# Graph layer and mixture of experts on one core: the results of the late tiles are scattered by node and choice and loaded with plain DMAs, and the first flush moves ahead by two slots

## The reference, cut to what matters

```python
def _L0_gnn_ref(h, edge_index, W, b):
    msg_sum = segment_sum(h[src], dst, num_segments=n)      # n = 6250 nodes, 100000 edges, rows of 256
    deg = segment_sum(ones, dst, num_segments=n)
    agg = msg_sum / maximum(deg, 1.0)[:, None]
    return concatenate([h, agg], axis=1) @ W.T + b

def _L0_ffn_ref(x, gamma, beta, Wr, br, W1, b1, W2, b2):
    xn = layernorm(x) * gamma + beta
    top_vals, top_idx = top_k(xn @ Wr + br, 2)              # 8 experts, each node goes to 2
    w = softmax(top_vals)
    for e in range(E):
        y_e = gelu(xn @ W1[e] + b1[e]) @ W2[e] + b2[e]      # 256 -> 512 -> 256
        y = y + y_e * w_full[..., e, None]
    return y

x = x + _L0_gnn_ref(_layernorm(x), edge_index, W, b)
x = x + _L0_ffn_ref(_layernorm(x), ...)
```

## Time and profile before

| | us |
|---|---|
| runs: median of 3 | 1417.49 (1415.44 to 1422.76) |
| profiled execution | 1415.15 |
| its span, first to last instruction | 1413.9 |
| busy: PE / DVE / ACT / POOL | 1139.6 / 809.4 / 462.6 / 950.6 |

### The profile page before, as it was taken

How to read it: one execution, slowest core, us unless ns; L and a number is a source line. 1 busy time by engine, 2 the same in 40 slices (tenths; PEclk the granted TensorE clock), 3 DMA queues, 4 the chain that set the end, 5 groups by cost and what they waited for, 6 DMA issues and landing times.

```text
span 1413.9 us, 23187 instructions
## 1 busy us (share of the span) xinstructions
PE 1139.6 (81%) x5743; PEld 878.7 (62%) x5743; DVE 809.4 (57%) x2583; ACT 462.6 (33%) x1017; POOL 950.6 (67%) x995
## 2 busy tenths in 40 slices
PE   3478798679768889888889988898898787899990
PEld 2234545457436767677767866776676566689980
DVE  8766645645644465555456546555776765652443
ACT  6200004113202433432252342343324333366650
POOL 3577777777777777777767776767675574205776
PEclk9999998889978999999999999999999988999995
DMA  8734655344334544444444543544444343235775
GB/s 269 231 107 135 215 182 167 118 131 136 117 119 128 153 131 146 144 136 140 141 128 127 151 139 121 152 123 132 153 139 117 111 136 98 78 110 156 227 222 150
DMA packets 125797, 205.43 MB, mean 145 GB/s; under 512 B 24491, under 2 KB 91844, under 8 KB 125540
## 3 DMA queue, kind: packets, MB, share of 16 engines
q0 software_dynamic: 48352, 129.18, 31.4%
q1 hardware_dynamic: 77188, 74.77, 16.2%
q10 hardware_dynamic: 128, 0.00, 0.0%
HBM read 160.19 MB, written 43.65 MB: 144 GB/s over the span
## 4 chain that ended last, share of the span: by engine, by line
PE 56%; DVE 14%; issue 10%; POOL 9%; ACT 7%; DMA 3%; DVEq 2%; ACTq 0%; POOLq 0%
PE psum L716 16%; PE psum L813 13%; PE psum L788 13%; PE psum L732 5%; POOL region L621 4%; DVE acc L1073 4%; POOL work L644 2%; POOL work L621 2%; PE psum L767 2%; PE psum L733 2%; DMA work<-h_rows,srcs 2%; ACT pay L567 1%; ACT expert_buf L594 1%; PE psum L800 1%; ACT region L535 1%
## 5 line engine op out<-in xcount | busy, mean ns | idle before, releaser
L621 POOL DMA_INDIRECT work<-h_rows,srcs x719 | 681.3, 948 | 264.6 <-issue 169.0
L1073 DVE TENSOR_TENSOR acc<-acc,psum 128x257 f32 x830 | 349.8, 421 | 406.9 <-PE psum L716 342.0
L716 PE MATMUL psum<-work 128*128 128x257 f32 x1438 | 445.6, 423 | 101.4 <-DVE acc L1073 77.8
L716 PEld LDWEIGHTS psum<-work 128*128 128x128 f32 x1438 | 256.3, 204 | 198.4 <-issue 140.4
L813 PE MATMUL psum<-region,expert_buf 128*128 x896 | 231.0, 404 | 9.8 <-ACT expert_buf L588 8.2
L594 ACT ACTIVATE expert_buf<-psum,b_col 128x128 f32<-128x128 f32 x448 | 127.9, 370 | 309.4 <-PE psum L788 309.1
L788 PEld LDWEIGHTS psum<-expert_buf 128*128 128x128 f32 x1792 | 219.9, 195 | 6.4 <-issue 1.7
L788 PE MATMUL psum<-expert_buf 128*128 128x128 f32 x1792 | 223.7, 279 | 0.0
L813 PEld LDWEIGHTS psum<-region,expert_buf 128*128 128x128 f32 x896 | 175.8, 204 | 43.7 <-issue 19.8
L948 DVE TENSOR_TENSOR work<-psum,rel 128x1152 f32<-128x1152 f32 x98 | 126.3, 1289 | 53.5 <-PE psum L716 31.2
L632 POOL DMA_INDIRECT queue<-pay,place_i x98 | 97.6, 996 | 84.4 <-DVE place_i L989 56.4
(11 more groups left out here) (242 smaller groups left out, 867.8 us busy)
## 6 DMA issues: line engine op xcount, KB each, us to landing
expert_buf<-queue SPq DMA_DIRECT2D x112, 128.0 KB
answers<-expert_buf SPq DMA_DIRECT2D x112, 128.0 KB
work<-h_rows,srcs POOLq DMA_INDIRECT x719, 2.8
region<-in_L_ffn_W_dram SPq DMA_DIRECT2D x16, 512.0 KB, 6.3
region<-in_x_dram SPq DMA_DIRECT2D x7, 896.0 KB, 11.5
h_rows<-region SPq DMA_DIRECT2D x7, 896.0 KB, 5.5
own<-h_rows SPq DMA_DIRECT2D x49, 128.0 KB
own<-in_x_dram SPq DMA_DIRECT2D x49, 128.0 KB
```

Of the source, the lines that this page charges most:

```text
L621: pool.indirect_dma_start(place_of(g)[:, 0:D], None, h_rows, bass.IndirectOffsetOnAxis(srcs[:, cell_of:cell_of + 1], 0)).then_inc(got[g % ...
L716: summed.up(pe.matmul(STEP_BANKS[t % BANKS][:, 0:GW], hot[:, k, :], rows, start=True, stop=True))
L1073: added.up(dve.tensor_tensor(sums, sums, STEP_BANKS[t % BANKS][:, 0:GW], ALU.add))
```

## The change

- SIZES and FLUSH: slots 37 to 48 are routed in four batches in place of five; the first half ends behind slot 36 (CUT = 37, 81 tiles), the second has 12 slots and 31 tiles. The values of t at which the 112 tiles begin are the same as before.
- Each queue row is longer by two numbers (ROW = 258): the node's number and its first choice of expert. DVE copies both into `pay` for each batch. Padding rows carry a number that points behind all nodes.
- For each tile of the second half DVE works out 128 destination rows (`destinations`): node number, plus OTHER where the tile's expert is not the node's first choice. POOL scatters the tile's results there (`parts`), in place of SP's store. Each scatter waits for the landing of the one before (`answered(pool, j - 1)`).
- The 12 late slots then need no gather: SP loads the first half of a slot's pair and ACT the second with plain DMAs (`fetch_part`), once all scatters have landed. The searches for the late slots (`results_rows`) go away.
- BACK, for slots 0 to 36, starts at t = 856 (before: 868); the late slots begin at t = 949 in both.

```diff
-    SIZES = [6, 6, 6, 5, 5, 5, 4, 2, 5, 3, 1, 1]
+    SIZES = [6, 6, 6, 5, 5, 5, 4, 6, 4, 1, 1]
...
-    FLUSH = 7
+    FLUSH = 6
...
-    ROW = D
+    ROW = D + 2
+    OTHER = NT * P
+    NOBODY = 2 * OTHER
...
+    parts = nc.dram_tensor("parts", (NOBODY + OTHER + P, D), F32).ap()
...
     def answered(engine, j):
-        if j >= 0:
+        if j >= FIRST_TILES:
+            engine.wait_ge(s_part[j % YB], 16 * late_before(j + 1, j % YB))
+        elif j >= 0:
             engine.wait_ge(s_answer, 16 * (j + 1))
...
                 qt_up.wait(sp, j - 2)
+                dest_up.wait(sp, j - 2 - FIRST_TILES)
                 row = sp.value_load(off_i[0:1, cell(j):cell(j) + 1], min_val=0, max_val=IDLE)
                 sp.dma_start(qrow[h], queue[ds(row, P), :]).then_inc(s_row[h], 16)
             for j in results(t - 2):
-                yb_up.wait(sp, j)
-                answered(sp, j - 1)
-                late = j >= FIRST_TILES
-                row = (j - FIRST_TILES * late) * P
-                sp.dma_start(answers[late][row:row + P, :], ysb[j % YB]).then_inc(s_answer, 16)
+                if j < FIRST_TILES:
+                    yb_up.wait(sp, j)
+                    answered(sp, j - 1)
+                    sp.dma_start(answers[j * P:(j + 1) * P, :], ysb[j % YB]).then_inc(s_answer, 16)
+            for r in backs(t):
+                if r >= CUT:
+                    fetch_part(sp, r, 0)
...
+    def fetch_part(engine, r, s):
+        row = engine.value_load(base_row[0:1, r:r + 1], min_val=0, max_val=(NT - 1) * P)
+        if r == CUT:
+            engine.wait_ge(s_blank, 16 * 2)
+            for k in range(YB):
+                engine.wait_ge(s_part[k], 16 * late_before(ALL_TILES, k))
+        if r < CUT + PAIRS:
+            whole_up.wait(engine, CUT - 1)
+        whole_up.wait(engine, r - PAIRS)
+        engine.dma_start(back(r, s), parts[s * OTHER:(s + 1) * OTHER, :][ds(row, P), :]).then_inc(s_late[r % PAIRS], 16)
...
+            for r in backs(t):
+                if r >= CUT:
+                    fetch_part(act, r, 1)
...
+            for j in results(t - 2):
+                if j >= FIRST_TILES:
+                    n = j - FIRST_TILES
+                    yb_up.wait(pool, j)
+                    dest_up.wait(pool, n)
+                    answered(pool, j - 1)
+                    pool.indirect_dma_start(parts, bass.IndirectOffsetOnAxis(dest_i[:, n:n + 1], 0), ysb[j % YB], None).then_inc(s_part[j % YB], 16)
             for r in backs(t):
+                if r >= CUT:
+                    continue
...
+        dve.tensor_copy(pay[:, b % 2, 0:n, D], tok[:, lo:hi])
+        dve.tensor_copy(pay[:, b % 2, 0:n, D + 1], e12[:, 0:n, 0])
         place_up.up(dve.tensor_tensor(place_i[:, b % 2, :, 0:n], place[:, :, lo:hi], trash[:, :, lo:hi], ALU.add))
...
+    def destinations(j):
+        n, c = j - FIRST_TILES, cell(j)
+        dve.wait_ge(s_row[j % 2], 16 * (j // 2 + 1))
+        dest_up.wait(dve, n - 2)
+        half_n = flip[:, n % 2:n % 2 + 1]
+        d_own.then(dve.tensor_scalar(half_n, qrow[j % 2][:, D + 1:D + 2], eq_[:, c:c + 1], float(OTHER), ALU.not_equal, ALU.mult))
+        dest_up.up(dve.tensor_tensor(dest_i[:, n:n + 1], half_n, qrow[j % 2][:, D:D + 1], ALU.add))
```

More of the change, by code:

```diff
@@ L122, in build @@
     QT = LISTED[NB]
+    SEARCHED = LISTED[FLUSH + 1]
+    LATE = ALL_TILES - FIRST_TILES
     OUT_ROWS = out.shape[0]
@@ L133, in build @@
     queue = nc.dram_tensor("queue", (QROWS, ROW), F32).ap()
-    answers = [nc.dram_tensor(f"answers{n}", (tiles * P, D), F32).ap() for n, tiles in enumerate((FIRST_TILES, ALL_TILES - FIRST_TILES))]
+    answers = nc.dram_tensor("answers", (FIRST_TILES * P, D), F32).ap()
+    parts = nc.dram_tensor("parts", (NOBODY + OTHER + P, D), F32).ap()
     def at(base, offset, *shape):
@@ L291, in build @@
     s_answer, s_pair = sem("s_answer"), [sem(f"s_pair{q}") for q in range(PAIRS)]
+    s_blank, s_late = sem("s_blank"), [sem(f"s_late{q}") for q in range(PAIRS)]
+    s_part = [sem(f"s_part{k}") for k in range(YB)]
     iotas, zcol_up, h_last, consts_up, fst_up, diag_up, less_up, ind_up, new_up, before_up = (
@@ L398, in answered, with late_before @@
     def answered(engine, j):
-        if j >= 0:
+        if j >= FIRST_TILES:
+            engine.wait_ge(s_part[j % YB], 16 * late_before(j + 1, j % YB))
+        elif j >= 0:
             engine.wait_ge(s_answer, 16 * (j + 1))
+    def late_before(n, k):
+        return sum(1 for j in range(FIRST_TILES, n) if j % YB == k)
     def results(t):
@@ L489, in sync_stream @@
                 sp.dma_start(queue[IDLE:IDLE + P, :], padrow[:, :]).then_inc(s_pad, 16)
+                for s in range(2):
+                    sp.dma_start(parts[s * OTHER + N:(s + 1) * OTHER, :], padrow[0:OTHER - N, 0:D]).then_inc(s_blank, 16)
             for b, blocks in ((FLUSH, 1), (NB - 2, 2)):
@@ L643, in gpsimd_stream @@
                 for s in range(2):
-                    pool.indirect_dma_start(back(r, s), None, answers[r >= CUT],
+                    pool.indirect_dma_start(back(r, s), None, answers,
                                             bass.IndirectOffsetOnAxis(answer_i[:, s, r:r + 1], 0)).then_inc(s_pair[r % PAIRS], 16)
@@ L1018, in tile_list @@
         d_own.up(dve.scalar_tensor_tensor(off_i[:, first:first + n], eq_[:, first:first + n], float(QUEUE), jtile[:, 0:n], ALU.mult, ALU.add))
-        d_own.up(dve.tensor_scalar(shift[:, first:first + n], iota[:, 0:n], float(P), float((UPTO[b] - (FIRST_TILES if b > FLUSH else 0)) * P), ALU.mult, ALU.add))
-        d_own.settle()
-        dve.tensor_scalar(tile_block[:, first:first + n], off_i[:, first:first + n], 1.0 / P, None, ALU.mult)
-        dve.tensor_tensor(shift[:, first:first + n], shift[:, first:first + n], off_i[:, first:first + n], ALU.subtract)
+        if b <= FLUSH:
+            d_own.up(dve.tensor_scalar(shift[:, first:first + n], iota[:, 0:n], float(P), float(UPTO[b] * P), ALU.mult, ALU.add))
+            d_own.settle()
+            dve.tensor_scalar(tile_block[:, first:first + n], off_i[:, first:first + n], 1.0 / P, None, ALU.mult)
+            dve.tensor_tensor(shift[:, first:first + n], shift[:, first:first + n], off_i[:, first:first + n], ALU.subtract)
         d_own.up(dve.tensor_scalar(ew_i[:, first:first + n], eq_[:, first:first + n], float(X - 1), None, ALU.min))
@@ L1034, in results_rows, with paired @@
     def results_rows(r):
-        cells = slice(0, LISTED[FLUSH + 1]) if r < CUT else slice(LISTED[FLUSH + 1], QT)
         for s in range(2):
-            i = dve.scalar_tensor_tensor(hit[:, s, cells], tile_block[:, cells], block[:, s, r:r + 1], shift[:, cells], ALU.is_equal, ALU.mult)
+            i = dve.scalar_tensor_tensor(hit[:, s, :], tile_block[:, :], block[:, s, r:r + 1], shift[:, :], ALU.is_equal, ALU.mult)
         d_own.then(i)
-        d_own.then(dve.tensor_reduce(found[:, :], hit[:, :, cells], AX_X, ALU.add))
+        d_own.then(dve.tensor_reduce(found[:, :], hit[:, :, :], AX_X, ALU.add))
         answer_up.up(dve.tensor_tensor(answer_i[:, :, r], place[:, :, r], found[:, :], ALU.add))
+    def paired(r):
+        if r < CUT:
+            dve.wait_ge(s_pair[r % PAIRS], 32 * (r // PAIRS + 1))
+        else:
+            dve.wait_ge(s_late[r % PAIRS], 32 * ((r - CUT) // PAIRS + 1))
+    def destinations(j):
[5 more added lines that the diff above has]
+        dest_up.up(dve.tensor_tensor(dest_i[:, n:n + 1], half_n, qrow[j % 2][:, D:D + 1], ALU.add))
     def vector_stream():
@@ L1046, in vector_stream @@
         dve.memset(shift[:, :], 0.0)
-        padrow_up.up(dve.memset(padrow[:, :], 0.0))
+        d_own.then(dve.memset(padrow[:, :], 0.0))
+        padrow_up.up(dve.tensor_scalar(padrow[:, D:D + 1], pcol[:, :], float(NOBODY), None, ALU.add))
         dve.tensor_copy(qbase[:, :], qbase_i[:, :])
@@ L1121, in vector_stream @@
                     tile_list(b)
-            for r in range(NT):
-                if t == (LISTS[FLUSH] + 2 + 3 * r if r < CUT else LISTS[NB - 1] + 1 + r - CUT):
+            for r in range(CUT):
+                if t == LISTS[FLUSH] + 4 + 3 * r:
                     results_rows(r)
+            for j in begins(t):
+                if j >= FIRST_TILES:
+                    destinations(j)
             for j in results(t - 1):
```

8 lines of the change are left out of this document (4 added, 4 removed).

## The result

| | before | after |
|---|---|---|
| runs: median (lowest to highest) | 1418.17 us of 4 (1415.44 to 1422.76) | 1454.07 us of 4 (1452.58 to 1459.46) |
| profiled execution, its span | 1415.15, 1413.9 | 1452.85, 1451.3 |

The changed kernel takes 1.026 times as long (95% interval 1.0225 to 1.0295). The forecast was 1441 us: right in sign and 13 us short (it had 24 us more than before, and 36 us came), with the measured time just inside its range.

The account below looks back on a forecast made before the run. POOL's queue was taken as the bound from gather 0 on; a 41.1 us longer tail less a 16.85 us earlier start gave net +24.3 us, a 1438.2 us span, 1441 us for the median, range 1425 to 1455.

Parts of the forecast that it names:

- gather 0 starts: Start of POOL's run: 14.85 us sooner from fewer first-half tiles, 2 us from the routing steps, so at 1266.9 us.
- 98 operations to the first of the seven: POOL's run: 74 gathers and 24 scatters at 1.275 us each, 125.0 us without a wait.
- six steps of the last seven scatters: End of POOL's queue: each scatter waits for the landing of the one before, 16.2 us in all.
- first load to last store: SP's queue of 12 late loads and 12 stores: 23 steps of 1.12 us, 25.8 us.
- I take 2 us net; bounds: 9 us gained, 3 us lost: Routing steps ahead of gather 0: one batch fewer returns at most 5.3 us of PE; 22 small DVE copies cost 3.3 us.
- 6 x 2.7 = 16.2 us: Last seven scatters: landing 2.4 us after start plus 0.28 us restart, six times; bounds 7.7 to 22.2 us.
- Inside the run that is hidden: Scatter landings in POOL's run cost nothing, as two or four gathers, 3.8 us at least, separate scatters.
- rival of scatters that wait inside the run: Twelve scatters in POOL's run each wait 1.4 us, 17 us in all; half gives 1450 us; chance 0.12.
- idle time inside the run: Sign of a wrong forecast: POOL idle inside its run would mean PE or landing is the bound.
- rival at transfer speed: Late loads and stores run at 226 GB/s, 20.9 us in place of 25.8: 1436 us; chance 0.10.
- rule that I weighed there: Last part: by the skill's rule transfers, not SP's issue, would set it, making the sum 5 us lower.
- Faster: POOL's operations follow without the 0.30 us gap, under 0.96 us each: 1409 us or 1403; chance 0.05.

Follow-up runs that it names:

- the three pairs above: Three kernels (new sizes alone, the changed kernel, the changed kernel with unchained scatters and row numbers read ahead), each with late and early searches; medians differ by 11.4, 10.5, 1.7 us.
- no_chain_b: The changed kernel with only the first scatter waiting and padding rows sent to rows of their own: 1431.18 us, 1.0141; on the slow chip 1.0105.
- both_fixes: The changed kernel with scatters that don't wait for each other and late row numbers read ahead: 1425.47 us, 1.0075.
- rows_ahead_b: The changed kernel with the 12 late row numbers read by one register load each on SP and ACT: 1443.26 us, 1.0183; on the slow chip 1.0041.
- cut33: both_fixes with the first half ending four slots earlier (33 slots, 66 gathers, 39 scatters): 1428.34 us, 1.0084.
- wide_rows: The kernel before with only the longer queue rows and two copies per batch: 0.9975 on the slow chip; 1418.45 us, 1.002 on another.
- sizes_only: The kernel before with only the new SIZES and FLUSH, results still gathered: 1.0006 on the slow chip; 1405.69 us, 0.9926 on another.

## Why the prediction was right or wrong

| term | forecast | after | off by |
|---|---|---|---|
| gather 0 starts | 1266.9 | 1272.7 | +5.8 |
| 98 operations to the first of the seven | 125.0 | 127.8 | +2.8 |
| six steps of the last seven scatters | 16.2 | 19.9 | +3.7 |
| last scatter to first load | 2.5 | 2.8 | +0.3 |
| first load to last store | 25.8 | 26.4 | +0.6 |
| last store to the end | 1.8 | 1.8 | 0 |
| span | 1438.2 | 1451.3 | +13.1 |

**What bounds the tail, right.** POOL's queue sets the time from gather 0 on, then the chain of scatters, then SP. Each was shown by removing it: without the scatters the runs lose 40.8 us, without the chain the trace loses 13.6 us in the chain's own terms (22.9 us between the runs), with rows read ahead the runs lose 10.8 us.

**"I take 2 us net; bounds: 9 us gained, 3 us lost": the step that failed.** The forecast had the steps end 2 us earlier than before, and allowed 3 us either way at gather 0; they ended 4.0 us later, and gather 0 came 5.8 us late. What was priced at nothing without a reason is the shift of the searches, which was not in the sum at all, although it is a line of the whole diff (quoted above) and the earlier trace rows shows gather 0 hanging on the end of the steps. It lengthened the stretch behind the 650th accumulation by 3 to 9 us, as the three pairs above show. The two pieces that the term did hold were both sized smaller than what the traces had: the missing batch and the new crowding gave 13.7 us, 9.5 of them behind the 650th accumulation, where the forecast let at most 5.3 us of PE come back; the two copies and longer rows cost 9.1 us on top of that, where 3.3 was forecast, though the runs have this only as 6.4 us and, alone, as none clear of their spread. That the pieces nearly cancel, and the term as a whole was off by only some 6 us, is luck. The mistake of kind is that small DVE operations in the steps were priced by their own duration (0.15 us each, and nothing for a shift). By which path they cost more was not shown; most of the shift's cost stands in the traces as slower matmuls at a lower granted clock, and that they lower it by holding up PE in DVE's order is my reading.

**"6 x 2.7 = 16.2 us", mis-sized.** The landing was right, 2.4 to 2.5 us, but the restart of 0.28 us had been read from a wait that DVE ended. Behind a landing it is 3.32 - 2.5 = 0.8 us. The term measured 19.9 us. The bounds (7.7 to 22.2) held it.

**"Inside the run that is hidden", nearly.** The rival of scatters that wait inside the run was right in kind: landings took up to 4.4 us, POOL stood 1.69 us at one scatter, and the chain cost 2.4 us there (no_chain_b), against the rival's 17. The idle time inside the run that the forecast named as a sign of being wrong is there, but small. PE's last matmul ended at 1408.35, where 1399 was forecast; 8.6 of these 9.4 us are the later start and the longer run, so the forecast of PE's pace stood, and the rows of after at 1358 us show the DVE wait behind it.

**SP's last part, right.** 1.15 us per step, by register read and issue, against 1.12. The rival at transfer speed (20.9 us) is refuted for after and gets its say once SP reads ahead: both_fixes takes 16.6 us to the start of its last store and 18.3 us to its end, at 250 GB/s where the rival reckoned with 226. On the rule that I weighed there (the Trainium skill, "DMA: Bandwidth & Descriptors", section on issuing engines not being separate DMA queues, that the time to issue is usually small beside the transfer): this case's trace disagrees for transfers whose row is read into a register first, whose issuing set the pace of 26.4 us.

**The other sign.** "Faster" asked for POOL operations under 0.96 us from start to start. They kept their gap: 125.4 / 98 = 1.28 us from start to start in no_chain_b, where no scatter waits for a landing. But the change does hold a faster kernel, which the forecast didn't look for: its first edit alone, at 1405.69 us.

**Left open.** Kernels with nearly the same code in the steps (after, no_chain_b, rows_ahead_b, both_fixes) end the steps 4.0 us later to 4.5 us earlier than before. A good part of that is there at the 650th accumulation, which kernels with the same instructions up to it reach up to 9.3 us apart, and was not taken apart. What sets the granted clock in the steps was not tried; the phase of the searches against the tiles may bear on it, and that is a guess. The 6.5 us that no_chain_b starts earlier than after are of this kind, and are not shown to come from the chain. How a second flush like cut33's would do without DVE's in-order wait was not tried.

## What to carry to other kernels

An operation moved off a gather must be priced with everything that its order asks for: here 24 gathers of 1.275 us became 31 scatters of the same price, plus a chain of landings and a queue of transfers that each read their row first, most of the 48 us that after takes over the new sizes alone. Small operations in the order of a busy stage can't be priced by their duration alone, and a shift of them is not free; read the diff for every number that moves them. Before a few us between two traces are put down to an edit, look at a point up to which both give the same instructions: what is there already is spread, here up to 9.3 us. And when a change consists of two parts that can be run apart, run them apart: the part thought of as preparation was the improvement.

## What the runs showed of the hardware

- One chip ran everything slower by a quarter. The kernel before took 1786.14 us there (median of 29), against 1416 to 1418 us on the others. The trace of wide_rows there has a mean granted clock of 0.836, where the runs on the other chips have 0.91 to 0.93, and waits that no instruction of the core explains:

```profile
PEld psum L716 <- issue: 416.4, 312, 8.3
...
DVE acc L1075 <- remote: 273.5, 75, 11.8
```

  The columns are total us, times, longest. The same kernels came out at other ratios there: rows_ahead at 1.0041 and elsewhere at 1.0183, no_chain at 1.0105 and 1.0141, sizes_only at 1.0006 and 0.9926. A comparison is worth what its chip is.
- POOL restarts 0.28 us after an engine's signal and about 0.8 us after a landing, by 3.32 us from start to start with landings of 2.5 us.
- Between executions of one kernel on one chip the mean granted clock and the time go together: before spans 1406.0 us at 0.932 and 1423.3 us at 0.917.
- With 37 small searches on DVE two program steps later, the stretch behind the 650th accumulation was 7.3, 6.3 (or 3.4) and 8.8 us longer in three pairs of kernels, of which 4.7, 5.3 and 8.1 us stand as longer busy time of PE for the same matmuls.
